# Vision tower on one Trainium2 core: the tiles of the expert layer, their gathers and sums begin one step sooner relative to the attention

## The reference

```python
emb = einsum('bnk,ek->bne', patches, W) + b + pos_embed          # 16 x 1024 x 64
xi = layernorm(h).reshape(n, 64, 1024)                           # read as channels x positions
K, Q, V = (Wk @ xi + bk, Wq @ xi + bq, Wv @ xi + bv)             # 8 heads of 8
ctx = softmax(K, over positions) @ V.T ; att = ctx.T @ softmax(Q, over the head's channels)
h = h + transpose(Wr @ att + br + xi)
...
probs = softmax(z @ gate_w + gate_b); top_probs, top_idx = top_k(probs, 2)   # normed to sum 1
hidden = silu(z @ w1[e]) * (z @ w2[e]); expert_out = hidden @ w3[e]
h = h + einsum('bseo,bse->bso', expert_out, dispatch)
```

## Time and profile before

| | |
|---|---|
| median of 3 runs | 757.75 us (753.18 to 760.39) |
| profiled execution: time, span | 757.5 us, 755.7 us |
| busy, share of the span | PE 82%, PEld 69%, POOL 67%, DVE 63%, ACT 47% |
| TensorE's granted clock over the span | 0.877 |
| indirect DMAs on POOL: scatters, of pieces, gathers, of pieces | 224, 16, 224, 16 |

### The profile page before, as it was taken

One profiled execution on the slowest core, in us unless ns is written; L12 is line 12 of the kernel. 1 busy time (PEld: TensorE's weight loads), 2 busy tenths in 40 slices (PEclk: granted clock), 3 DMA queues, 4 the chain that ended last, 5 costly groups with the idle time before them and its releaser, 6 DMA issues.

```text
span 755.7 us, 13960 instructions
## 1 busy us (share of the span) xinstructions
PE 622.1 (82%) x4059; PEld 519.8 (69%) x4059; DVE 476.6 (63%) x1322; ACT 353.2 (47%) x774; POOL 503.5 (67%) x537
## 2 busy tenths in 40 slices
PE   5886687788979998999889998998894888799328
PEld 3365454666568967886779687967884787798228
DVE  5654645567556677767666756766585687598410
ACT  2121311226355647564656456545562557486400
POOL 4362044757577477777777777777777777777773
PEclk9958778589989999999999989998998789898755
DMA  3499504134184329542844284537351635664322
GB/s 82 90 175 345 203 29 111 49 108 120 56 226 132 95 55 230 136 131 65 208 134 131 62 204 120 135 82 165 92 149 57 164 98 158 175 150 98 68 59 59
DMA packets 169200, 94.52 MB, mean 125 GB/s; under 512 B 99551, under 2 KB 153207, under 8 KB 169129
## 3 DMA queue, kind: packets, MB, share of 16 engines
q1 hardware_dynamic: 152728, 67.65, 34.5%
q0 software_dynamic: 15616, 25.59, 12.8%
q10 hardware_dynamic: 784, 0.39, 0.2%
HBM read 45.40 MB, written 48.18 MB: 124 GB/s over the span
## 4 chain that ended last, share of the span: by engine, by line
PE 51%; DVE 20%; issue 9%; POOL 7%; DMA 6%; ACT 5%; ACTq 0%; SPq 0%; POOLq 0%; DVEq 0%
PE h_ps L1593 8%; PE wide_ps L1381 7%; PE y_ps L1614 5%; PE hidT_ps L1606 4%; PE turn_ps L1571 3%; PE wide_ps L1401 3%; DMA hx<-xi_scratch 2%; PE wide_ps L1504 2%; DVE twice_y L1298 2%; POOL rows_scratch L674 2%; POOL kexp L691 2%; POOL hx L691 2%; DMA xi_scratch<-xi 2%; PE wide_ps L1387 2%; ACT sums L860 2%
## 5 line engine op out<-in xcount | busy, mean ns | idle before, releaser
L674 POOL DMA_INDIRECT rows_scratch<-z_parts,place x224 | 224.5, 1002 | 126.9 <-issue 64.9
L691 POOL DMA_INDIRECT sums<-y_scratch,place x192 | 185.1, 964 | 66.2 <-issue 56.4
L1593 PE MATMUL h_ps<-w_hi,rowsT 128*128 (+1 forms) x388 | 117.8, 330 | 15.8 <-DVE hid_all L1300 15.4
L1298 DVE SCALAR_TENSOR_TENSOR twice_y<-tanh,h_ps 128x256 f32<-128x256 f32 (+1 forms) x194 | 80.4, 414 | 52.5 <-ACT tanh L818 31.2
L1593 PE MATMUL h_ps<-w_lo,rowsT 128*128 (+1 forms) x388 | 105.6, 298 | 0.0
L1614 PE MATMUL y_ps<-w_sb,hidT_all 128*128 (+1 forms) x776 | 103.1, 279 | 1.4 <-ACT twice_y L833 1.4
L1614 PEld LDWEIGHTS y_ps<-w_sb,hidT_all 128*128 128x128 f32 (+1 forms) x776 | 100.2, 202 | 2.3 <-issue 2.3
L1593 PEld LDWEIGHTS h_ps<-w_hi,rowsT 128*128 128x128 f32 (+1 forms) x388 | 78.8, 203 | 25.9 <-issue 22.3
L818 ACT ACTIVATE tanh<-h_ps 128x256 f32<-128x256 f32 (+1 forms) x194 | 69.6, 386 | 46.5 <-PE h_ps L1593 42.6
L1300 DVE SCALAR_TENSOR_TENSOR hid_all<-twice_y,h_ps 128x256 f32<-128x256 f32 (+1 forms) x194 | 81.6, 421 | 6.7
L1571 PE MATMUL turn_ps<-ident,rows_all 128*128 128x128 f32 (+1 forms) x388 | 64.4, 292 | 21.0 <-DMA rows_all<-rows_scratch 14.2
(11 more groups left out here) (350 smaller groups left out, 1107.0 us busy)
## 6 DMA issues: line engine op xcount, KB each, us to landing
rows_all<-rows_scratch SPq DMA_DIRECT2D x84, 256.0 KB
y_scratch<-twice_y SPq DMA_DIRECT2D x84, 128.0 KB
rows_scratch<-tanh SPq DMA_DIRECT2D x3, 3276.0 KB
xi_scratch<-xi SPq DMA_DIRECT2D x16, 256.0 KB
hx<-xi_scratch SPq DMA_DIRECT2D x14, 256.0 KB
rows_scratch<-z_parts,place POOLq DMA_INDIRECT x224
out<-sums SPq DMA_DIRECT2D x56, 64.0 KB
x_in<-in_x SPq DMA_DIRECT2D x26, 128.0 KB
```

The costliest lines, as they stand in the source:

```text
L674: gp.indirect_dma_start(rows_dram[n], bass.IndirectOffsetOnAxis(ap=place[m % RING][:, r, j:j + 1], axis=0), z_parts[m % 2][:, j // 2, j % ...
L691: gp.indirect_dma_start(y_of[r][apart(m)][:, j // 2, j % 2, :], None, y_dram[m % 3][0:GROUPS[m] * GROUP * width(m), :], bass.IndirectOffse ...
L1298: ve.scalar_tensor_tensor(twice[0:w, j, :], tanh[0:w, j, :], 1.0, halves[:, j, 0, :], ALU.add, ALU.mult).then_inc(S["twice_done"], 1)
L1593: mm = te.matmul(h_ps[0:w, j * 256:(j + 1) * 256], rowsT[g % 2][:, j * w:(j + 1) * w], w12[:, bass.ds(experts[g][j], 1), :, :].rearrange(" ...
```

## The change

LAG goes from 23 to 22: every operation of a group stands one step sooner, with the same order inside a step. The table of sums goes down by one throughout, the table of gathers by one, that of pair 0 by two. The attention, the scatters and the pieces keep their steps. POOL's gate goes with LAG.

```diff
-LAG = 23
+LAG = 22
...
-GATHER = (38, 51, 65, 78, 91, 102, 111, 123)
-SUMS = ([[43 + 14 * m + q for q in range(4)] for m in range(5)]
-        + [[112, 113, 114, 115], [121, 122, 122, 123], [124, 125, 126, 127]])
+GATHER = (36, 50, 64, 77, 90, 101, 110, 122)
+SUMS = ([[42 + 14 * m + q for q in range(4)] for m in range(5)]
+        + [[111, 112, 113, 114], [120, 121, 121, 122], [123, 124, 125, 126]])
```

## The result

The changed kernel takes 761.28 us (median of 10 runs, 759.24 to 765.20) where the kernel before, timed beside it, takes 755.42 (751.71 to 760.39): a ratio of 1.0086, 95% interval 1.0056 to 1.0116. It is 5.9 us slower. That is inside the predicted range of 751.0 to 763.0 and within 1%, but the forecast was no change, and the interval excludes that. The profiled execution took 764.0 us, its span 762.3, TensorE's granted clock over the span 0.866 (0.877 before).

What follows compares the result with a forecast made beforehand. POOL's queue was taken to set the end from 253.76 us on. The head start of 5.4 us, less 2.3, 1.5 and 1.6, left 0.0: forecast 757.5 us, no change, range 751.0 to 763.0.

Steps and rivals of the forecast that it cites:

- What bounds the kernel: From 253.76 us on, POOL's queue of 384 indirect DMAs sets the end; PE, though busier, runs ahead.
- Rival B: PE is the bound and only e is added: 759.7 us; chance 0.12.
- e: Time the first group costs PE at the start, making every attention event later: 2.2 us, bounds 1.1 and 4.
- Rival D: PE waits for rows before the query product, so tiles don't start sooner; e 3.6, time 760.3 us; chance 0.08.
- The head start: POOL's first gather, of pair 0, waits for y of group 11 and starts at 248.4: gain 5.4 us.
- Pair 3's slots: POOL's scatter of pair 3 waits for slots written at 291.1, starting at 291.4: gain left 3.1 us.
- the gate at pair 4: Pair 4's scatter in step 59 waits for PE's transposes until 374.2, starting at 374.5: gain left 1.6 us.
- The four gathers: Four DMAs ahead of pair 6's last scatters delay rows 5.0 us; piece 12 ready at 638.3: gain left 0.
- rival A: The head start is kept, if e is small and gates open earlier: 752.1 us, at the extreme 749.8; chance 0.19.
- Rival C: Slower at pair 7's pieces: PE's longer stop brings one more stretch of half clock, 762.5 us; chance 0.17.
- That everything behind the pieces has slack: After pair 7's pieces nothing more is lost: y of the last group at 706.18 + 5.0 against 725.52.

Runs made afterwards that it cites:

- Without the pick (experiment): Changed kernel with pair 7's pick on DVE moved ahead of the multiply in the same step: 757.80 us, ratio 1.0018 to the kernel before.
- the kernel before with a stop of 14.26 us: Kernel before with only pair 4's gather one step sooner (90 for 91): 754.72 us, ratio 0.9981.
- The kernel with e cut, the gate loosened and both repairs at the stop: Changed kernel, pair 4's gather one step later, pair 7's pick before the multiply, group 0's transposes behind the query product, looser POOL gate: 752.53 us, ratio 0.9943.
- the kernel before with two small edits: Kernel before with pair 0's gather one step sooner (37) and POOL's gate one group looser: 751.72 us, ratio 0.9955.
- the first: Changed kernel with pair 4's gather one step later again (91), behind pair 6's scatter: 759.81 us, ratio 1.0063 to the kernel before.

## Why the prediction was wrong, by its own steps

*What bounds the kernel: right.* POOL's queue stayed the chain from the first gather to the end. The loss stands in it as waits at the pieces, all but 0.6 us, and no wait of POOL's has grown after the pieces: y of the last group was copied where 714.02 stands in the row below, against POOL's coming for it at 732.07. Rival B fell with that. Timeline of ACT, changed kernel:

```profile
714.02 0.36 ACT L833 ACTIVATE twice_y<-y_ps 126x256 f32<-126x256 f32 x1
```

*e: 2.2 predicted, 3.5 measured* (slots of pair 2, 107.9 against 104.5), inside the bounds of 1.1 to 4. The rows landed near where I said, at 157.68 less the 1.0 between the executions, 156.7 against 156.4. What was dearer is the work behind: windows of the changed kernel,

```profile
157.00:158.00 1.00, 0.32 (x2) 0.33 (x3) 0.39 (x1) 0.38 (x1) 0.00 (x0) 0.50 1.12 336
...
160.00:161.00 1.00, 0.92 (x3) 0.20 (x1) 0.04 (x1) 0.00 (x0) 0.00 (x0) 0.50 0.78 226
```

and of the kernel before:

```profile
157.00:158.00 1.00, 0.23 (x2) 0.00 (x0) 0.70 (x2) 0.00 (x0) 0.69 (x2) 1.00 0.96 305
```

The query product ended at 160.93, which is 2.7 us later than before on the common count, and not 1.4. The 1.2 us between come from four places: the rows 0.3 us later; the transposes 0.76 us to the next start (157.68 to 158.44) where I had 0.60; the product 1.91 us where I had 1.67; and, the largest, 0.58 us (158.44 to 159.02) of a product that my sum left out. That is the bias product (L1398), which the new order has between the transposes and the query product; before, it started at 154.77, ahead of the product that I timed from 155.56. All but the rows would have been shorter had the clock come to 1.00 as before. The other 0.8 of e has the size that I had put for the work ahead of attend.

Rival D named nearly these numbers (e 3.6, gains left of 1.7 and 0.2; measured 3.5, 1.4 and 0.2) by a condition that didn't hold: it had PE wait for all three loads, to about 158.2, and the rows came at 156.7. Its match is luck in the main (of the query product's 2.7 us of lateness more than half has other causes than the wait for rows, which took 1.21 us), and its 3 us at piece 12 is too little by 3.7.

*The head start: 5.4 predicted, 3.9 measured.* POOL's own scatter of pair 2 was the last to be ready, not y: the gather follows it after the usual 0.30. That scatter is e later. The mechanism held, the size is e's.

*Pair 3's slots: gain left 3.1 predicted, 1.4 measured; the gate at pair 4: 1.6 predicted, 0.2 measured.* The waits are the two forecast, by the same releasers: 2.77 for slots (2 predicted) and 0.94 for transposes (1.5 predicted). The steps between took 2.5 and 1.2 where I had 2.3 and 1.5. What was too high is the start, by e. Between there and the first piece the queue regained 1.5 us that I hadn't counted.

*The four gathers: this is the step that failed.* I predicted that piece 12 would be ready at 638.3 and cost 1.6, bounds 3 more. It was ready at 643.3 on before's count, 12.3 us later than before where I had 7.3, and the waits at the pieces took 6.7 (12.3 of lateness, less the 7.3 of room that could be used there, plus the 1.7 that POOL came early). With 1.7 in hand ahead of the first of them and 0.6 lost in small amounts, that makes the 5.6. The piece was 5.0 us later than I had said, in three parts: 0.4, 2.6 and 2.0.

- The release of PE was close: 590.3 on before's count, 589.9 predicted.
- The recovery was not. I let the three steps behind the stop run as the earlier trace rows show them, 3.25, 4.64 and 3.90, 11.8 us in all, and had attention 7.3 us late at step 95. They took 2.86, 7.00 and 4.56, 14.4 us, and attention was 10.3 late. I had shifted the stop by a step without asking what stands beside it on the *other* engines. On DVE the pick of pair 7 stood ahead of the stop, free before, and now costs 4.1 at step 95. Without the pick (experiment) the three steps take 10.1 us and attention is 6.2 late: so my prices of the bare steps were 1.7 us too high, and part of what I forgot was hidden by that.
- From step 95 to the pieces I put further lateness at nothing, and it was 2.0, of which 1.7 in step 99 (7.2 us against 5.5). It is there in every kernel with the new table of sums and in none with the old one. I had thought of the sums' shift only as something that could help (rival A). That the sums are its cause is argued from the rows, not tried.

*Rival C had the place and the test right* (the waits at the pieces passed 4 us, 762.5 forecast, 761.3 measured), *but not the cause.* Its half clock for one stretch more isn't what the stop brings: in the kernel before with a stop of 14.26 us the steps behind it are as short as behind 10.49. A half clock did take part, in the second place: it came back after PE ran dry behind the pick. By the rows of PE, release to step 94 is 9.86 us (591.34 to 601.20) against 7.29 without the pick (591.02 to 598.31), 2.6 more for the pause, and step 94 then took 4.56 against 2.80 us, 1.8 more, nearly all of it at 0.50 to 0.65: together 4.3, the pick's price to within 0.2.

*That everything behind the pieces has slack: right.* *Rival A* needed a small e and gates that open early. The kernel with e cut, the gate loosened and both repairs at the stop is at 0.9943, 4.3 us of gain in 755, of the 5.4 that A named: a gain of that size is there to be had, but not by this change alone, and it doesn't need this change: the kernel before with two small edits is at 0.9955.

*Two statements about the numbers themselves were off.* I took 1% for what a measurement can tell from no change; the interval was 0.3% to either side, so a loss of 0.8% could be seen. And the chances don't fit together: I left some 0.09 outside the range at each end but gave 0.11 and 0.10 to being more than 1% off, which lies further out still.

## What to carry to other kernels

When a table of steps is shifted for one kind of work and not for another, look at every long stall and write down, for each engine, what is queued on either side of the instruction that will wait it out. Work that was free inside the stall can fall behind it and cost its full length, though nothing is added, and the engine that pays need not be the one that waits. List every operation that the new order puts in front of the one you time, and price it at the clock that the engine will have behind a pause. And when two repairs each help, run the kernel with neither, each and both, and compare the part of the trace that both edits can reach: here that showed costs that add up where the theory had them only together.

## What the runs showed of the hardware

A pause of PE of 1.21 us in front of the rows at 157.68 was followed by 0.50 of granted clock up to 161, where before it, with the product running through, the clock had come to 1.00 from 157 on. And at 599 to 601 us two microseconds without a matmul, at a clock of 1.00, were followed by 0.65 and 0.50. The Trainium skill ("TensorE: Matmul & The Clock Gate", Part 1) has the clock throttled by default and released by activity; the rows agree in both directions. What I had not expected is the cost of the short pauses. At 1.00 the same query product takes 1.03 us, as later in the kernel before:

```profile
229.12 1.03 PE L1401 MATMUL wide_ps<-proj_qv,hx 128*128 128x256 f32 x4
```

There the bias product ahead of it takes 0.32 us to the next start (228.80 to 229.12), and four transposes take 0.55 (160.50 to 161.05). So of the 3.25 us from 157.68 to 160.93 at most 1.35 is the half clock (3.25 - 0.55 - 0.32 - 1.03); this is an estimate, since before, too, the clock rose only at about 156.9. Step 94 would have been 1.8 us shorter. Behind the long stop the clock came back alike whatever its length: 0.62 in the microsecond to 594.00 after a stop of 10.49 us that ended at 586.54, 0.85 in the microsecond to 600.00 after one of 14.26 us that ended at 592.53, about 7 us behind the release both times. In the kernel before, lengthening it cost nothing.

The first scatters of profiled executions of these kernels lie 3.7 us apart, more than most effects looked for here. Counting from an event ahead of the change made the profiles agree with the medians for the change itself (5.6 and 5.9 us), though not for every experiment (for the first, 2.3 us slower than before in the profile and 4.8 by the medians).
